# A macaron transformer on one core: when O's two banks are summed, where two normalisings and a gated product's split run, and what a moments wait holds up

## The reference

```python
x = x + 0.5 * ffn(layernorm(x))      # two layers
x = x + ttt(layernorm(x))            # a linear memory, scanned over 512 steps
x = x + 0.5 * ffn(layernorm(x))      # the same two layers again

def layer(x):                        # shift: second half of the features from the row before
    q, k, v = split(shift_token(x) @ wqkv, 3)          # 8 heads of 64
    q, k = rotary_xpos(l2norm(q) * qs, l2norm(k) * ks)
    x = x + local_attention(q, k, v) @ wo              # 128 keys back, window 128
    h = (shift_token(x) - mean) / sqrt(var + 1e-5) * lg + lb
    a, g = split(h @ w1 + b1, 2)                       # 682 each
    return x + (a * gelu(g)) @ w2 + b2
```

## Time and profile before

| | before |
|---|---|
| median of 3 runs | 2625.47 us (2623.58 to 2627.92) |
| the profiled execution | 2626.11 us, span 2624.2 us |
| TensorE busy | 2528.5 us, 96% of the span, clock granted 0.999 |
| VectorE busy | 1991.5 us, 76% |
| ScalarE busy | 1821.3 us, 69% |
| GpSimd busy | 1551.2 us, 59% |
| VectorE's wait for GpSimd's `xb` | 58.9 us, 30 times |

### The profile page before, as it was taken

The page is one execution under the profiler, slowest core; times in us unless marked ns, Lnnn a source line. Parts: engine busy times, 40 slices in busy tenths (PEclk is TensorE's granted clock), DMA queues, the critical chain, the costliest instruction groups (busy, mean ns, idle before and its releaser), DMA issues.

```text
span 2624.2 us, 79930 instructions
## 1 busy us (share of the span) xinstructions
PE 2528.5 (96%) x29664; PEld 2235.5 (85%) x29664; DVE 1991.5 (76%) x6533; ACT 1821.3 (69%) x5192; POOL 1551.2 (59%) x1767
## 2 busy tenths in 40 slices
PE   8999999999999999999999899999999999999999
PEld 7888888888888888888777788888888888888888
DVE  7787777777777777777656787777777788778786
ACT  6777777777777776766454777667677677767775
POOL 6666666656656665665212566666656666666655
PEclk9999999999999999999999999999999999999999
DMA  3122011003000000005101000000003100000000
GB/s 122 34 82 78 18 46 54 26 20 118 14 2 3 2 2 26 2 2 198 39 18 34 2 2 2 2 2 2 2 2 117 36 2 18 18 18 18 18 18 26
DMA packets 75954, 82.18 MB, mean 31 GB/s; under 512 B 37552, under 2 KB 61872, under 8 KB 74416
## 3 DMA queue, kind: packets, MB, share of 16 engines
q1 hardware_dynamic: 70176, 75.51, 8.8%
q10 hardware_dynamic: 5392, 1.56, 0.2%
HBM read 49.53 MB, written 26.74 MB: 29 GB/s over the span
## 4 chain that ended last, share of the span: by engine, by line
PE 40%; DVE 22%; POOL 16%; issue 9%; ACT 8%; DMA 3%; SPq 1%; DVEq 0%; POOLq 0%; ACTq 0%
POOL pr L634 9%; DVE pr L1728 6%; PE bank L1359 5%; PE bank L1125 5%; PE bank L1127 4%; PE bank L1126 4%; PE bank L1161 4%; PE bank L1236 4%; DMA stt<-stt 3%; DVE t L1691 3%; DVE t L1694 3%; ACT pr L821 3%; POOL r L618 3%; PE bank L1188 3%; PE bank L1524 2%
## 5 line engine op out<-in xcount | busy, mean ns | idle before, releaser
L634 POOL TENSOR_TENSOR pr<-pr,rden 128x384 f32<-128x384 f32 (+1 forms) x512 | 436.2, 859 | 457.1 <-DVE rden L1737 456.2
L821 ACT ACTIVATE pr<-pr,nb 128x192 f32<-128x192 f32 (+1 forms) x1024 | 438.2, 430 | 162.3 <-DVE nb L1728 162.3
L1125 PE MATMUL bank<-h2T,w 128*128 128x256 f32 x1408 | 405.4, 288 | 4.9 <-DVE h2T L1763 1.2
L1126 PE MATMUL bank<-h2T,w 128*128 128x256 f32 x1408 | 395.1, 281 | 0.0
L1127 PE MATMUL bank<-h2T,w 128*128 128x256 f32 x1408 | 395.1, 281 | 0.0
L1728 DVE CUSTOM_DVE_ANT_0 pr<-bank,maskb,r 128x192 f32<-128x192 f32 (+1 forms) x1024 | 352.3, 396 | 37.6 <-issue 26.4
L666 POOL TENSOR_TENSOR uTl<-t,uTh 128x256 fp32r<-128x256 f32 x288 | 219.9, 764 | 200.7 <-ACT uTh L921 199.9
L1825 DVE SCALAR_TENSOR_TENSOR t<-bank,b,t 128x256 f32<-128x256 f32 (+1 forms) x384 | 184.3, 481 | 178.2 <-ACT t L906 102.9
L1125 PE MATMUL bank<-wqkv,hT 128*128 128x512 f32 x768 | 307.2, 400 | 3.4 <-DVE nb L1728 2.6
L1126 PE MATMUL bank<-wqkv,hT 128*128 128x512 f32 x768 | 302.8, 394 | 0.0
L1127 PE MATMUL bank<-wqkv,hT 128*128 128x512 f32 x768 | 299.8, 390 | 0.0
(11 more groups left out here) (244 smaller groups left out, 7059.3 us busy)
## 6 DMA issues: line engine op xcount, KB each, us to landing
wqkv<-wqkv_split SPq DMA_DIRECT2D x18, 512.0 KB, 6.3
w<-w_split SPq DMA_DIRECT2D x3, 2816.0 KB, 9.8
Y<-in_x SPq DMA_DIRECT2D x8, 512.0 KB, 7.5
out<-Y SPq DMA_DIRECT2D x8, 512.0 KB, 3.6
stt<-stt SPq DMA_DIRECT2D x224, 3.0 KB
h<-out SPq DMA_DIRECT2D x7, 512.0 KB, 4.0
out<-h SPq DMA_DIRECT2D x7, 512.0 KB, 3.0
stt<-stt SPq DMA_DIRECT2D x192, 0.0 KB
```

Source lines behind the costliest of these rows:

```text
L634: e.tensor_tensor(probs(j, t), probs(j, t), rden[:, 2 * j:2 * j + 2].unsqueeze(2).to_broadcast([P, 2, w]), ALU.mult).then_inc(pn_done, 1)
L821: last = e.activation(probs(j, t)[:, g, :], probs(j, t)[:, g, :], ACT.Exp, bias=nb[:, hd:hd + 1], scale=-1.0, accum_out=den[:, hd:hd + 1])
L1125: e.matmul(out, left[0], right[0], start=first, stop=False)
L1126: e.matmul(out, left[0], right[1], start=False, stop=False)
```

## The change

- `O_first(t)`, `O_add(t)` and ScalarE's `O(t)` now stand at the end of tile t (ScalarE: the first copies ahead of `A2`, `O` behind it). VectorE's `O(t - 1)` stands ahead of `S` of tile t. `WO` keeps its place.
- In tile 0 the normalisings of pairs 2 and 3 are VectorE's (`NP_first`, a semaphore of their own), and VectorE's order there is new; ScalarE makes the k square between pairs 1 and 2. The k rotary no longer waits for GpSimd's low part of u, the q rotary does, and each rotary of tile 1 waits for the square of the same bank.
- `U_last` moves from VectorE to GpSimd, ahead of the first `NP`.
- `LN_moments(2)` stands behind `U(0, 1)` instead of ahead of it.
- In tiles 1 and 2 `halves` stands ahead of `A0`. The two guard semaphores become one.

```diff
 # GpSimd
-                e.tensor_scalar(ssg[:, 0, :], ssk[:, :], 1e-24, None, ALU.max).then_inc(guard_k, 1)
-                e.wait_ge(guard_k, at(guard_k, m + 1))
+                e.tensor_scalar(ssg[:, 0, :], ssk[:, :], 1e-24, None, ALU.max).then_inc(guarded, 1)
+                e.wait_ge(guarded, at(guarded, 2 * m + 1))
...
-                                rden[:, 2 * j:2 * j + 2].unsqueeze(2).to_broadcast([P, 2, w]), ALU.mult).then_inc(pn_done, 1)
+                                rden[:, 2 * j:2 * j + 2].unsqueeze(2).to_broadcast([P, 2, w]),
+                                ALU.mult).then_inc(pn_done, 1 if t or j == 0 else 3)
+
+            def U_last(L, b):
+
+                f = 8 * L + b
+                e.wait_ge(u_done, at(u_done, 12 * f + 12))
+                e.wait_ge(u_hi, at(u_hi, 12 * f + 11))
+                e.tensor_copy(uTh[:, 1, JOBS[-1], :], ut[:, 1, :]).then_inc(u_hi, 1)
+                e.wait_ge(u_hi, at(u_hi, 12 * f + 12))
+                e.tensor_tensor(uTl[:, 1, JOBS[-1], :], ut[:, 1, :], uTh[:, 1, JOBS[-1], :], ALU.subtract).then_inc(u_lo, 1)
...
-                    for j in range(4):
+                    if prev and t == 0:
+                        U_last(*prev)
+                    for j in range(4 if t else 2):
                         NP(L, b, t, j)
...
 # ScalarE
-                    if t > 1:
-                        O_first(L, b, t - 1)
-                    for j in range(3):
+                    for j in range(4):
                         S(L, b, t, j)
-                        if t and j == 0:
-                            O(L, b, t - 1)
-                    if t == 0:
-                        A1_k(*ahead)
-                    S(L, b, t, 3)
+                        if t == 0 and j == 1:
+                            A1_k(*ahead)
...
+                    if t:
+                        O_first(L, b, t)
                     if t == 3:
-                        O_first(L, b, t)
                         O(L, b, t)
                     if ahead:
                         A2(*ahead)
+                    if t < 3:
+                        O(L, b, t)
...
 # TensorE, PT
-                e.wait_ge(pn_done, at(pn_done, 4 * n + j + 1))
+                if t or j < 2:
+                    e.wait_ge(pn_done, at(pn_done, 4 * n + j + 1))
+                else:
+                    e.wait_ge(pn_first, at(pn_first, 2 * (8 * L + b) + j - 1))
...
 # VectorE, rotary
-                    if t == 1:
-                        e.wait_ge(u_hi, at(u_hi, 12 * (8 * L + b)))
-                        e.wait_ge(u_lo, at(u_lo, 10 * (8 * L + b)))
+                elif t == 1:
+                    e.wait_ge(u_hi, at(u_hi, 12 * (8 * L + b)))
+                    e.wait_ge(u_lo, at(u_lo, 10 * (8 * L + b)))
...
+                if t == 1:
+                    e.wait_ge((sqk, sqq)[i], at((sqk, sqq)[i], m + 1))
...
+            def NP_first(L, b, j):
+
+                n = idx(L, b, 0)
+                e.wait_ge(rden_done, at(rden_done, 4 * n + j + 1))
+                e.tensor_tensor(probs(j, 0), probs(j, 0),
+                                rden[:, 2 * j:2 * j + 2].unsqueeze(2).to_broadcast([P, 2, 2 * HB]), ALU.mult).then_inc(pn_first, 1)
...
 # VectorE, sequence
-                    if t > 1:
-                        O_add(L, b, t - 1, 0)
+                    if t:
+                        O(L, b, t - 1)
                     S(L, b, t, 0)
-                    if t > 1:
-                        O_add(L, b, t - 1, 1)
                     S(L, b, t, 1)
                     S(L, b, t, 2)
                     R(L, b, t, 0)
                     S(L, b, t, 3)
-                    if t:
-                        O(L, b, t - 1)
...
+                    if t == 0:
+                        R(L, b, t, 1)
+                        rotary(*ahead, 0)
+                        squares(idx(*ahead), 0)
+                        R(L, b, t, 2)
+                        NP_first(L, b, 2)
...
+                        R(L, b, t, 3)
+                        NP_first(L, b, 3)
+                        rotated(*ahead, 0)
+                        rotary(*ahead, 1)
+                        rotated(*ahead, 1)
+                        squares(idx(*ahead), 1)
+                        if L == 0 and b < B - 1:
+                            for j in range(1, 4):
+                                entry_stats(b + 1, j)
...
+                        A0(*ahead2)
+                    else:
...
                         if t < 3:
                             halves(L, b, t - 1)
+                        if ahead2:
+                            A0(*ahead2)
+                        for i in pair:
+                            O_add(L, b, t, i)
...
-                        for i in pair:
-                            O_add(L, b, t, i)
                         LN_apply(L, b, 0)
...
                     if mt == 0:
                         LN_apply(L, b, 1)
+                    if mt == 1:
                         LN_moments(L, b, 2)
-                    if mt == 1:
                         U_rest(L, b, 0)
```

More of the change, by code:

```diff
@@ L1710, in squares @@
             def squares(m, i):
[L1712 removed]
+                squared, sums, summed = ((sqk, ssk, ssk_done), (sqq, ssq, ssq_done))[i]
                 e.wait_ge(squared, at(squared, m + 1))
[L1714 removed]
+                e.wait_ge(guarded, at(guarded, 2 * m - 1 + i))
                 e.tensor_reduce(sums[:, :], sq[:, i, :].rearrange("p (h d) -> p h d", h=HEADS), AX.X, ALU.add).then_inc(summed, 1)
@@ L1941, in sequence @@
                     S(L, b, t, 3)
[L1942 to L1959 removed]
+                    if t == 0:
[4 more added lines that the diff above has]
+                        NP_first(L, b, 2)
+                        if L == 0 and b == 0:
+                            entry_apply(0, 2)
+                        R(L, b, t, 3)
[7 more added lines that the diff above has]
+                                entry_stats(b + 1, j)
+                        if L == 0 and b == 0:
+                            no_neighbour()
+                        A0(*ahead2)
+                    else:
+                        for j in range(1, 4):
+                            if L == 0 and b == 0 and t == 1 and j == 2:
+                                entry_apply(0, 3)
+                            R(L, b, t, j)
+                            if ahead and j == 1:
+                                rotary(*ahead, 0)
+                            if ahead and j == 2:
+                                rotated(*ahead, 0)
+                        if ahead:
+                            squares(idx(*ahead), 0)
                         WO(L, b, t - 1)
@@ L1963, in sequence @@
                             halves(L, b, t - 1)
-                        squares(idx(*ahead), 1)
-                        rotary(*ahead, 1)
-                        rotated(*ahead, 1)
-                    elif ahead:
-                        A1(*ahead)
-                    if L == 0 and b < B - 1 and t == 0:
-                        entry_stats(b + 1, 3)
-                    if L == 0 and b == 0 and t == 3:
-                        beta()
-                    if L == 0 and b == 0 and t == 0:
-                        no_neighbour()
-                    if ahead2:
-                        A0(*ahead2)
-                    if t:
-                        if not ahead:
-                            WO(L, b, t - 1)
-                            LN_moments(L, b, 0)
-                            halves(L, b, t - 1)
+                        if ahead:
+                            squares(idx(*ahead), 1)
+                            rotary(*ahead, 1)
+                            rotated(*ahead, 1)
+                        if L == 0 and b == 0 and t == 3:
+                            beta()
                         if t < 3:
                             halves(L, b, t - 1)
+                        if ahead2:
+                            A0(*ahead2)
+                        for i in pair:
+                            O_add(L, b, t, i)
                     if L == 0 and b == 0 and t < 3:
@@ L2055, in transformer @@
                     sequence(L, B - 1, (L, B - 2), None if last else (L + 1, 0))
-                for part in range(2):
-                    U_last(L, B - 1, part)
                 for t in range(NT):
```

35 lines of the change are left out of this document (5 added, 30 removed).

## The result

The changed kernel takes 2656.4 us (median; 2656.1 to 2658.7), the kernel before 2624.5 us (2623.2 to 2627.9) on the same chip: ratio 1.0121, 95% interval 1.0104 to 1.0139. It is 1.2% slower. The direction was forecast, the size was not: 2656.4 lies above 2633.1 and above the top of the range, 2648. The later runs were made on several chips; the kernel before took 2623.4 to 2628.1 us beside them, so the ratio to it says more than a time.

What follows compares the result with a forecast made beforehand. Sequences were taken as bound by TensorE (busy 96%) nearly throughout. Plain sequences +11.0, layer 0 -1.4, those without `prev` -2.5, ends +0.5: total +7.6 us on the median 2625.5, giving 2633.1 us, range 2605 to 2648.

Steps and rivals of the forecast that it cites:

- First tile and second tile's chain: TensorE's QKV of the second tile, behind VectorE's first-tile order, starts later: +1.3 us a plain sequence, bounds 0.95 and 1.9.
- `O` at its tile's end, on ScalarE and in tiles 2 and 3: ScalarE's first copies cost 0.1 us a sequence; earlier probability transposes in tiles 2 and 3 gain 0.54.
- Last gated job on GpSimd: Two instructions moved to GpSimd's idle time before the first normalising: no cost, except +0.5 us in all at the transformers' ends.
- Layer 0 and the ends: First-tile chain costs only +0.6 us in layer 0's six sequences; transformers' ends, where the last `xb` waits, +0.5 in all.
- a tile stage without `prev`: Two sequences with no `xb` or W2 to wait for keep the first tile's gain of 0.4 us.
- Second gated product ahead of moments: In the gated stage it runs during the statistics' DMA wait, bringing h2's normalising sooner: -0.4 us a sequence, bounds 0 and -0.6.
- the gains don't show: Rival: TensorE's waits at transposes and h2 turn into a wait for ScalarE's q copy: 2663 us, chance 0.06.

Runs made afterwards that it cites:

- experiment 5: Changed kernel with VectorE's `O` of tile 0 put back behind `S` of tile 1: 2638.9 us, ratio 1.0060.
- experiment 2: Kernel before with only `LN_moments(2)` moved behind `U(0, 1)`: 2644.5 us, ratio 1.0083.
- Experiments 3 and 4: Changed kernel with GpSimd's second low part of u (3), or both (4), waiting for VectorE's h2 normalisings: 2652.6 us (3), 2660.8 us (4).
- experiment 1: Changed kernel with only `LN_moments(2)` put back ahead of `U(0, 1)`: 2645.3 us, ratio 1.0086.
- experiment 12: Changed kernel with all four first-tile normalisings on GpSimd again and the previous sequence's `xb` ahead of the A1 of k: 2704.0 us, ratio 1.0299.
- experiment 7: Changed kernel with all four normalisings of the first tile back on GpSimd: 2680.5 us, ratio 1.0200.
- experiment 6: Changed kernel with VectorE's squares of q put back ahead of the rotary of q: 2633.1 us, ratio 1.0019.

## Why the prediction was wrong, point by point

- **First tile and second tile's chain: right.** QKV of the second tile starts 12.23 us after the last k product (1835.94 less 1823.71); 12.2 was forecast. Of TensorE's wait 0.89 is for the addition of W2 and 0.63 for `nb`, where about a microsecond for `nb` was forecast. In layer 0 QKV starts 0.66 later (14.79 after the Exp load, 14.13 before); 0.6 was forecast. By links, on the clock of before: rotary of k 1808.31 (forecast 1808.2), end of the q squares 1814.60 (1814.35), `xb` 1816.65 (1816.35), W2 addition 1817.48 (1817.1), `S` 1818.48 (1818.1), QKV 1819.38. The two normalisings and their reciprocals took 1.09 (1.0 taken). One collision showed, as taken: the q sum at 0.89 beside the k product.
- **`O` at its tile's end, on ScalarE and in tiles 2 and 3: right.** The transposes take 1.04 in all three, and TensorE comes 0.27 and 0.25 sooner behind them. Ahead of `S` of tiles 2 and 3 it idles 0.18 instead of 0.12, until ScalarE's q copy, which is 0.12 for both (0.1 taken). `O` of tile 0 in the chain was priced at 0.68 and is worth 0.55 (experiment 5).
- **Last gated job on GpSimd: right.** Its two instructions take 0.40 and 0.74, and the first normalising starts where it did (1823.71 less 16.56 is 1807.15).
- **Layer 0 and the ends: small misses in the other direction.** The tile part of layer 0 was forecast at 0.6 + 0.1 - 0.54 = +0.16; the six are 0.04 to 0.7 shorter, about 0.4 each. The ends were put at +0.5 and a tile stage without `prev` at -0.84; the stretch with the middle and one such stage gave 1.0 back, the start and the end of the program changed by about 0.1. Tile stages, middle and ends together: forecast +19.9 + 0.5, measured 16.5 - 1.0.
- **Second gated product ahead of moments: the step that failed.** The prediction took -0.4 a sequence, bounds 0 and -0.6; it is +0.6 by the stage, and 21 us when made alone (experiment 2). Against the forecast's -12.8 the gated stages measured +14.9: 27.7 us off, more than the whole error of 23. The step priced the time at which the root is ready (1792.43) against the start of the normalising (1792.91), and took every duration as it stood. Two went up. The root took 1.08 instead of 0.85, and with that the normalising starts 0.13 sooner, not 0.48. VectorE's subtraction for the last rows of u (`U_rest`, 0.42) runs beside the root in both kernels. With the second product moved ahead of the moments it starts 0.05 ahead of the root (1882.53, 1882.58); before, it started 0.38 behind the root's start (1791.96, 1791.58). All kernels with the moments moved have the root at 1.08 in the median, all others at 0.85. And the earlier product gave GpSimd its second low part just when the normalising began: 1.63 instead of 0.87. Experiments 3 and 4 show that this is the low parts' doing, and that without it the transposes would end 0.14 sooner.
- The prediction weighed collisions for the first tile alone, and there only for VectorE instructions with two inputs in SBUF. The h2 normalising has one. By the Trainium skill (GPSIMD Engine Reference, Key points) GpSimd also contends with VectorE instructions in a 2-port performance mode, and by the Trainium skill (VectorE: DVE Perf Modes, section "Mode 2×_2P") an fp32 `tensor_scalar` from SBUF to SBUF is of that kind. The trace agrees: 0.34 alone, up to 0.77 beside a low part.
- The sizes follow what was left. In these traces the instruction that starts second is late by what is left of the first, less a little. The first normalising starts with 0.60 of a low part left and takes 0.35 more, the second with 0.68 left and takes 0.43 more: less 0.25 each time. In the kernel before the first one starts with 0.28 left (the low part ends at 1793.19, the normalising starts at 1792.91) and takes 0.03 more, so its collision does not show in the 0.87. The timelines of GpSimd and, for the root below, of VectorE:
```profile
1792.46 0.73 POOL L666 TENSOR_TENSOR uTl<-t,uTh 128x256 fp32r<-128x256 f32 x1
```
```profile
1791.96 0.42 DVE L1830 TENSOR_TENSOR uTh<-t,uTh 42x256 fp32r<-42x256 f32 x1
```
GpSimd behind a VectorE instruction with two inputs in SBUF is late by what is left less 0.14: the root of the changed kernel has 0.37 of `U_rest` left and takes 0.23 more; in the kernel before it started first and took 0.85. By the Trainium skill (SBUF — State Buffer, "SBUF: two separate sides") whichever instruction starts first holds the shared pair to its end and the other waits. The trace agrees, but for the 0.14 and 0.25. The rows of before show the 0.14 already: the power that takes 1.94 instead of 1.67 starts at 1813.99 with 0.42 of the addition left (1813.72 + 0.69). So both terms could have been priced from who starts first and what is left then.
- The rivals: "the gains don't show" had 2663 at 0.06, nearest in time and wrong in mechanism: the transposes did gain. None of the rivals had the gated stage getting slower.

## What to carry to other kernels

When an instruction is moved forward, list what else comes forward with it and what the other engine will run beside it: where VectorE and GpSimd took turns they may now overlap, and the durations of the old trace don't hold. Ask of each such pair which one starts first and how much of it is left when the other starts. Where a chain sets the end, look for work in it that it doesn't need (here `xb`, behind a root that it doesn't use) and put it into idle time further up, and only where there is idle time: the same edit gave 1.74 us a stage in one order and cost 1.24 in another. Price each mend in the order in which it will stand: the early squares gained 0.79 a stage with a late `xb` and cost 0.37 with an early one.

## What was not expected of the hardware

- TensorE's clock. The same two waits stand in the changed kernel (0.89 and 0.63) and in experiment 1 (0.90 and 0.62), in 24 sequences each. In the first the granted clock fell behind them in one sequence, in the second in six, at 1.57 us each; in experiment 12, behind a wait of 2.0 us, in about half of the sequences; in experiment 7, behind one of 1.32 us, in none. Why in one sequence and not in the next is open; no run separates it.
- GpSimd is slowed beside VectorE's sums as well, its small instructions most: its guard of 128x8 went from 0.24 to 0.78 beside a sum of 128x512 (0.68 left of it), its product from 1.04 to 1.43 (0.53 left), and its root, 1.67 alone, took 2.18 in experiment 6 beside the q sum (0.65 left). Each time it is what was left less 0.14; in the kernel before 94 normalisings of 128x384 that start with about 0.58 of a sum left take 0.44 more.
- Two GpSimd low parts took 1.41 beside three VectorE normalisings and 1.43 without them. All of that collision's cost was VectorE's: the first low part had started first, and the second started with 0.12 of a normalising left.
